# A decoder layer on one core: transpositions with 128 columns, and another order of values, keys, output projection, self scores and the second self output

## The reference

```
x = layernorm(x + self_attention(x))        # 16 "heads" of 16; batched over entries and heads,
                                            # with rotary position terms, softmax over 112 keys
x = layernorm(x + cross_attention(x, ctx))  # layernorm with gain and offset, 16 heads of 64,
                                            # softmax over 375 keys, output * tanh(gate)
x = layernorm(x + moe(x))                   # 8 experts, top 2, swiglu, plus a shared expert
```

## Time and profile before

| | |
|---|---|
| time, 3 runs | 716.70, 719.34, 722.49 us (median 719.34) |
| the profiled execution | 719.09 us |
| its span in the profile | 717.3 us |
| PE busy in the span | 592.4 us (83%) |
| one entry in the steady part, from R0 to R0 of the next | 53.94 us |
| the attention block's steps, 8 entries | from about 105 to 530 us |
| the experts | 530 to 717 us |

### The profile page before, as it was taken

One profiled execution on the slowest core, in us unless ns is written; L12 is line 12 of the kernel. 1 busy time (PEld: TensorE's weight loads), 2 busy tenths in 40 slices (PEclk: granted clock), 3 DMA queues, 4 the chain that ended last, 5 costly groups with the idle time before them and its releaser, 6 DMA issues. The chain is left out here.

```text
span 717.3 us, 14307 instructions
## 1 busy us (share of the span) xinstructions
PE 592.4 (83%) x4746; PEld 462.2 (64%) x4746; DVE 478.0 (67%) x903; ACT 408.7 (57%) x995; POOL 268.4 (37%) x296
## 2 busy tenths in 40 slices
PE   4733788999999989989989989999759878899980
PEld 3523566777777777778778777777546564566650
DVE  3895446877877876876876876876747786733332
ACT  2445337567567567567567567565517546644431
POOL 3462023344344344344354354333412741333332
PEclk9965788999999999999999999999966999999995
DMA  8625110210210210210210210310307576333324
GB/s 221 227 101 177 29 49 30 50 51 15 64 49 14 65 51 6 72 43 15 70 41 17 71 40 15 112 59 35 103 30 264 163 246 227 64 59 54 60 30 110
DMA packets 58069, 57.34 MB, mean 80 GB/s; under 512 B 17266, under 2 KB 47218, under 8 KB 58034
## 3 DMA queue, kind: packets, MB, share of 16 engines
q1 hardware_dynamic: 53650, 50.89, 23.1%
q0 software_dynamic: 4384, 5.99, 5.0%
HBM read 46.74 MB, written 10.13 MB: 79 GB/s over the span
## 5 line engine op out<-in xcount | busy, mean ns | idle before, releaser
L652 POOL TENSOR_TENSOR c_rcp<-c_sum,neg_one 112x2 f32<-112x2 f32 x64 | 44.5, 696 | 203.4 <-ACT probs L795 203.4
L656 POOL TENSOR_TENSOR probs<-probs,c_rcp 112x750 f32<-112x750 f32 x64 | 92.0, 1437 | 5.0
L795 ACT ACTIVATE probs<-ps_s,c_neg 112x375 f32<-112x375 f32 x128 | 72.6, 580 | 22.8 <-DVE c_neg L1027 22.3
L687 ACT ACTIVATE kt_hi<-ps_o 128x376 fp32r<-128x376 f32 x64 | 31.8, 497 | 68.3 <-PE ps_o L151 68.3
L1658 POOL DMA_INDIRECT moe_sum<-gsh_hi,xs_in x21 | 34.2, 1628 | 79.4 <-ACT gsh_hi L1709 64.7
L1031 DVE SCALAR_TENSOR_TENSOR cpt_lo<-ps_t,cpt_hi 125x672 f16<-125x672 f32 x64 | 54.4, 850 | 13.0 <-ACT cpt_hi L802 13.0
L1022 DVE SCALAR_TENSOR_TENSOR v_lo<-ps_vx,v_scale,v_hi 125x512 f16<-125x512 f32 x48 | 35.9, 749 | 40.3 <-ACT v_hi L787 39.9
L1347 PE MATMUL ps_t<-ident,probs 112*125 112x112 f32 x384 | 54.4, 280 | 8.8 <-DVE cpt_lo L1031 8.7
L1027 DVE TENSOR_REDUCE c_neg<-ps_s 112x2 f32<-112x750 f32 x64 | 59.4, 929 | 1.1 <-PE ps_s L151 1.1
L1971 PE MATMUL ps_h<-w_ex,xst_hi 128*128 (+1 forms) x168 | 58.0, 387 | 2.5 <-DVE xst_lo L1748 2.4
L1347 PEld LDWEIGHTS ps_t<-ident,probs 112*125 112x125 f32 x384 | 50.4, 195 | 12.6 <-POOL probs L656 7.5
(11 more groups left out here) (312 smaller groups left out, 1796.9 us busy)
## 6 DMA issues: line engine op xcount, KB each, us to landing
chunk<-in_L_ffn_ew_dram SPq DMA_DIRECT2D x24, 512.0 KB, 3.6
spare<-in_L_ffn_ew_dram SPq DMA_DIRECT2D x18, 512.0 KB, 6.1
store<-in_L_ffn_ew_dram SPq DMA_DIRECT2D x6, 512.0 KB, 5.3
ctx_all<-in_ctx_dram SPq DMA_DIRECT2D x2, 1500.0 KB
ctx_raw<-in_ctx_dram SPq DMA_DIRECT2D x8, 375.0 KB
moe_in<-chunk SPq DMA_DIRECT2D x1, 2709.0 KB, 14.1
plain_raw<-in_L_xattn_w_kv_dram SPq DMA_DIRECT2D x2, 1024.0 KB, 15.2
xs_in<-moe_in SPq DMA_DIRECT2D x15, 129.0 KB, 2.1
```

What stands on the lines that cost most here:

```text
L652: pool.tensor_tensor(c_rcp[:, s % 2, :], c_sum[:, s % 2, :], neg_one[:, :], ALU.pow).then_inc(sg["c_rcp_ready"], 1)
L656: pool.tensor_tensor(p, p, r, ALU.mult).then_inc(sg["p_normed"], 1)
L795: act.activation(probs[:, s % 2, h, :], ps_s[0:N, h, 0:SK], ACT.Exp, bias=c_neg[:, s % 2, h:h + 1], accum_out=c_sum[:, s % 2, h:h + 1]).th ...
```

## The change

The fills of the next entry and the steps keep their work. What differs:

1. The six transpositions of `p_transpose` take 128 columns of the probabilities instead of 125 (three of them belong to the next third, or to a zeroed margin at the end), and write 128 partitions. The four of `self_pt` take 128 instead of 112 columns. What comes out beyond 125 and 112 is not read.
2. At steps 3 and 6 (`V_FIRST`) `v_project` stands ahead of `k_project` on PE, and on ACT and DVE the same; on ACT `exps(s)` stands ahead of both. Fill place 1 comes behind them.
3. At step 2 PE does `cross_out` ahead of fills S2 and S3, and DVE does `k_lo` and `x2_moments` ahead of their maxima.
4. O1 moves from the end of step 3 to place 0 of step 4.
5. Two waits are added that the new order needs: for the low part of the context ahead of V00, and once for the zeroed margin.

```
-           (3, 2): ["T3"], (3, 4): ["O1"], (5, 1): ["OT", "C0"], (5, 3): ["C1", "PJ"],
+           (3, 2): ["T3"], (4, 0): ["O1"], (5, 1): ["OT", "C0"], (5, 3): ["C1", "PJ"],
+V_FIRST = (3, 6)
...
-        probs = sb("probs", [N, 2, 2, SK])
+        probs = sb("probs", [N, 2, 2, SK + P - SKT])
-        e_self = work[:, 0:2 * B * N].rearrange("p (s n) -> p s n", s=2 * B)
+        e_self = work[:, :].rearrange("p (s n) -> p s n", s=2 * B)
...
+            pool.memset(probs[:, :, :, SK:], 0.0).then_inc(sg["p_padded"], 1)
...
 ACT:
-                    if s == 2:
+                    if s == 2 or s in V_FIRST:
                         exps(b, s)
                     place(0)
+                    if s in V_FIRST and v_here(b, s, more):
+                        v_hi_cross(b if s < 6 else b + 1, V_AT[s])
                     if s + 2 < PAIRS:
                         k_hi(b, s + 2)
                     elif more:
                         k_hi(b + 1, s + 2 - PAIRS)
-                    if s in (3, 7):
+                    if s == 7:
                         exps(b, s)
                     place(1)
-                    if s not in (2, 3, 7):
+                    if s not in (2, 7) and s not in V_FIRST:
                         exps(b, s)
...
-                    if v_here(b, s, more):
+                    if s not in V_FIRST and v_here(b, s, more):
                         v_hi_cross(b if s < 6 else b + 1, V_AT[s])
...
 DVE:
-                    if s == 2:
-                        place(1)
-                    else:
+                    if s != 2:
                         place(0)
+                    if s in V_FIRST and v_here(b, s, more):
+                        v_lo_cross(b if s < 6 else b + 1, V_AT[s])
                     if s + 2 < PAIRS:
                         k_lo(b, s + 2)
                     elif more:
                         k_lo(b + 1, s + 2 - PAIRS)
                     if more and s == 0:
                         stack_lo(b + 1)
-                    if s != 2:
-                        place(1)
                     if s == 2 and later(b):
                         x2_moments(b - 1)
+                    place(1)
...
 PE:
-                    last = pe.transpose(bank(f"T{i}")[0:N, j * N:(j + 1) * N], e_self[:, 4 * i + j, :], ident[0:N, 0:N])
+                    last = pe.transpose(bank(f"T{i}")[:, j * N:(j + 1) * N], e_self[:, 4 * i + j, :], ident[0:N, 0:N])
...
+                if f == "V00":
+                    pe.wait_ge(sg["ctxt_lo"], 2 * b + 2)
...
+                if not later(b) and s == 0:
+                    pe.wait_ge(sg["p_padded"], 1)
...
-                        last = pe.transpose(ps_t[0:SKT, h, t * N:(t + 1) * N],
-                                            probs[:, s % 2, h, t * SKT:(t + 1) * SKT], ident[0:N, 0:N])
+                        last = pe.transpose(ps_t[:, h, t * N:(t + 1) * N],
+                                            probs[:, s % 2, h, t * SKT:t * SKT + P], ident[0:N, 0:N])
...
                     place(0)
+                    if s in V_FIRST and v_here(b, s, more):
+                        v_project(b if s < 6 else b + 1, V_AT[s])
                     if s + 2 < PAIRS:
                         k_project(b, s + 2)
                     elif more:
                         k_project(b + 1, s + 2 - PAIRS)
-                    place(1)
                     if s == 2 and later(b):
                         cross_out(b - 1)
-                    if s != 2 and v_here(b, s, more):
+                    place(1)
+                    if s != 2 and s not in V_FIRST and v_here(b, s, more):
                         v_project(b if s < 6 else b + 1, V_AT[s])
```

More of the change, by code:

```diff
@@ L653, in normalise @@
                 pool.wait_ge(sg["c_rcp_ready"], PAIRS * b + s + 1)
-                p = probs[:, s % 2]
+                p = probs[:, s % 2, :, 0:SK]
                 r = c_rcp[:, s % 2].unsqueeze(2).to_broadcast([N, 2, SK])
@@ L715, in self_exp @@
                 for j in range(4):
-                    last = act.activation(e_self[:, 4 * f + j, :], bank(f"S{f}")[0:N, j * N:(j + 1) * N], ACT.Exp,
+                    last = act.activation(e_self[:, 4 * f + j, 0:N], bank(f"S{f}")[0:N, j * N:(j + 1) * N], ACT.Exp,
                                           bias=s_neg[:, f, j:j + 1])
@@ L794, in exps @@
                 for h in range(2):
-                    act.activation(probs[:, s % 2, h, :], ps_s[0:N, h, 0:SK], ACT.Exp, bias=c_neg[:, s % 2, h:h + 1],
+                    act.activation(probs[:, s % 2, h, 0:SK], ps_s[0:N, h, 0:SK], ACT.Exp, bias=c_neg[:, s % 2, h:h + 1],
                                    accum_out=c_sum[:, s % 2, h:h + 1]).then_inc(sg["c_exp"], 1)
```

## The result

The changed kernel takes 785.30 us (median of 4, 784.75 to 787.40) against 720.91 us for the kernel before in the same runs: ratio 1.0901, 95% interval 1.0851 to 1.0951. That is 64 us slower. The forecast was 765 us, the range 736 to 783: the side was right, the size too small by 20 us, and the time lies above the range. The profiled execution is the one of 784.75 us. In two later kernels one execution stood far above the rest (1375 us of six in the one with the sum first, 791 us of ten in the one with O1 late and idle work), and the ratios leave these out.

What follows compares the result with a forecast made beforehand. PE sets the pace, with little room at hand-overs from DVE and ACT. Seven entries at 5.4 us (37.8) plus 1.4 for the last take 719.09 to 758.3; 7 for the clock gives 765 us, range 736 to 783.

Steps and rivals of the forecast that it cites:

- Transpositions: Six p_transposes of 128 columns: 0.16 us gained an entry; the self part nothing, at worst 0.8 us.
- the ends 0 and 4.6 us: Limits of the transpositions' gain in all; 4.6 us if PE were never stopped behind them.
- The rival that the loads stay slow: The start address, not the 125 columns, makes loads slow; 766 us, chance 0.02, inside the forecast's range.
- Step 2: cross_out ahead of S2, S3: gain 0 of 1.0 us hoped for; T0 waits for exponentials, ACT and DVE 0.6 us late.
- Step 3 and O1: O0's sum behind values and keys: T3 waits 2.7 us; O1's late values make OT 3.75 us late.
- Step 6: Low keys come behind V00, so pv waits 2.3 us; R0 starts 1.9 us later, after the normalised x's low part.
- The sum without the clock: 3.65 + 1.9 - 0.16 = 5.4 us for each of seven entries, last entry + 1.4; 719.09 + 39.2 = 758.3 us.
- The clock: PE's new waits bring stretches at 1.2 GHz, up to three an entry: 0 to 24 us in all, 7 taken.
- Fewer waits: Rival: one of the waits isn't there or is half; 734 to 752 us, chance 0.22.
- Faster: Rival: V11 and V00 fill PE's waits for DVE, DVE's and ACT's lists miss nothing; 698 or 708 us, chance 0.10.
- its own condition: At step 6, low keys done when PE finishes NT (about 309), that is, exps(6) able to start 2.3 us earlier.
- no change: Rival: nothing to measure, gains and waits cancelling; 719 us, chance 0.04.

Runs made afterwards that it cites:

- the one with the sum first: Against the kernel before: 128-column transpositions, cross_out ahead of S2 and S3 on PE, on DVE the residual sum alone ahead of their maxima; 713.15 us, ratio 0.9851.
- the one with O1 late and idle work: Against the kernel before: O1 at the start of step 4 and 14 unread transpositions ahead of OT; 731.28 us, ratio 1.0140.
- The kernel with idle work in the waits: Changed kernel plus transpositions nobody reads: 8 ahead of T0, 22 of T3, 14 of OT, 22 of step 6's pv; 757.96 us, ratio 1.0533.

## Why the prediction came out as it did

**Transpositions.** The load fell to 141 ns as read off, and the time didn't move (0.9997). Of the ends 0 and 4.6 us it is the lower one, within the interval. The rule of the Trainium skill ("TensorE: Matmul & The Clock Gate", LDWEIGHTS), by which the wider load would cost an estimated 1 to 3 us, is refuted in sign by the rows (189 to 141 ns); the total can't tell its 1 us from nothing. The rival that the loads stay slow falls with the rows.

**Step 2.** Forecast: no gain, T0 waits, ACT and DVE 0.6 us late. Right: T0 waits 1.07 us, and the part alone costs 3.4 us.

**Step 3 and O1.** Forecast: T3 waits 2.7 us; measured 2.39 us of idle, which with the matmul that is still running before it is much the same wait. The chain from maxima(3) to the sum is 4.60 us, as added up (4.6). OT's wait is there, but only in three of the six entries in the window above. In the other three the lower clock behind T3 lasts 10.2 us and has stretched step 4; both kinds of entry take 63 us.

**Step 6.** 3.04 us measured, 3.06 forecast: right, and so is the wait of pv. The last link was wrong. The forecast had R0 wait for the low part of the normalised x, 0.94 us of DVE. With the clock kept up this took 0.39 us (0.94 before, beside work of POOL; why it fell wasn't tested), and PE came to R0 only at 334.73 us, without a wait, because pv, scores and keys ahead of it were late:

```profile
334.00 0.39 DVE L922 TENSOR_TENSOR xnt_lo<-xnt_f,xnt_hi 128x224 fp32r<-128x224 f32 x1 [0.47 <-ACT xnt_hi L763]
```

**The sum without the clock** was 758.3 us. The kernel with idle work in the waits, which keeps the clock up, measured 757.96 us. Counted from R0, against the kernel before, its T3 comes 2.2 us later (forecast 2.4), OT 3.5 (3.75), NT 3.5 (3.65), the pv of step 6 5.75 (5.95), and the next R0 5.2 us (5.4): 59.1 us an entry. So the waits were right piece by piece. That the totals agree to 0.3 us is in part luck: the entries are a little shorter than forecast, the last entry longer (its last scores come 2.6 us later, forecast 1.4), and the start differs by 1.8 us.

**The clock** is the step that failed: "between 0 and 3.5 us an entry, 0 to 24 in all. I take 1 us an entry, 7 in all". It costs 785.30 - 757.96 = 27.3 us, 3.9 us an entry, above its own upper bound. The mechanism was named, the places too; the term was too small, for two reasons. First, the forecast had up to three places of 3.4 us, 10.2 us an entry, and let only part of them count; the lower level lasted 13.7 us an entry, since behind T3's wait it held on for 10.2 us in every second entry while PE was busy. Second, the value of 1 us rested on "after each wait part of the work hides behind the next one", and no row stood behind its size. Part does hide: 13.7 us at half the clock would cost up to 6.9 us by estimate, and 4.0 were measured (63.1 against 59.1). But more than half went through, and not the small part that was taken.

**Rivals.** "Fewer waits" is refuted: all four are there, that of OT in half of the entries. "Faster" is refuted too, by its own condition: ACT's exps(6) waits for c_neg in the profile after (3.03 us), as it did before. So is "no change".

## What to carry to other kernels

In engines that work off fixed lists, moving a piece on the bounding engine is only half of the change: ask for each list which entry has a reader waiting, and put the one whose reader comes first in front. Values ahead of keys on PE cost 50 us with the lists of ACT and DVE turned too, and 3 us without. With `cross_out` first on PE, cutting one DVE helper in two, the part that PE waits for first, turned a ratio of 1.0025 into 0.9851 (with wide transpositions, which changed nothing alone). And a wait of PE can cost more than its length: here the matmuls at the lower clock behind the waits cost 3.9 us an entry, about 0.3 us for each us at the lower level. How long that level lasts has to be read from the new trace; idle work in the wait is a cheap way to measure what it costs.

## What the runs showed of the hardware

- A load of 125 columns of float32 for a transposition took 189 ns, of 128 columns 141 ns and of 112 columns 134 ns, at full clock. Those of 125 and 128 columns read the same tile; its rows became 3 elements longer with the change, so only the first three of twelve slices start at the same place, and they show the same step (never under 184 ns, never over 144 ns).
- 66 added transpositions in an entry, in PE's waits, made the kernel 27.3 us faster; the granted clock from 150 to 480 us was 0.89 without and 1.00 with them. Transpositions of float32 were thus enough to keep the clock up.
- The three stretches at the lower level in the entry shown each followed one in which PE was idle for nearly half or more (busy for 1.01, 1.80 and 1.07 us of 3.40). In other entries the lower level lasted 10.2 us behind such a stretch, with PE busy.
